# An adaptive-mixing, attention and expert kernel on one core: mixing and transposes in row halves, low parts and the second bound on GpSimd, new instruction orders

## The chip, the core and the metric

The kernel runs on one core of a Trainium2 chip. The core has TensorE (PE: matmuls, with its weight loads shown apart as PEld), VectorE (DVE), ScalarE (ACT), GpSimd (POOL) and SyncE (SP), which here only issues DMAs. Each engine works off its own list of instructions strictly in the written order, and waits at semaphores that other engines count up. The metric is the device time of one execution in microseconds; the median of the runs shown is compared.

## The reference, cut to what matters

The input x has 32 samples of 32 tokens with 512 columns.

```
att  = softmax(MLP(cond_128))                    # 8 shares per sample
x1   = einsum(att-weighted 32x32 weights, x) + bias            # mixing, per sample
q,k,v = x1 @ sign(W).T * (mean|W| * scale)       # 512, 128 and 128 columns, nan_to_num
a    = softmax(q k^T / 4) v                      # 32 heads, 8 kv heads, 32 tokens per sample
y    = a @ sign(Wo).T * (mean|Wo| * scale)       # nan_to_num
x1   = x + y
c    = grouped conv over columns (9 taps) of x1, + context + bias
out  = x1 + experts(c)                           # top 2 of 8 low-rank experts, gated
```

## The kernel before

The 1024 rows (sample, token) are held as 8 tiles t of 128 rows, and in the first part as 4 pairs i of tiles. There is no loop on the chip: each engine's list is written out by hand as calls of small functions, and the order of these calls is the order of the engine's instructions. The stages are:

- Mixing. `mix(i, b)` on TensorE multiplies the rows of x with block-diagonal weights (`agg_diag`); `full_mixed` on VectorE adds the bias into `mixed`; `high_part` on ScalarE rounds it to `mixed_hi`, `low_part` on VectorE takes the rest, `mixed_lo`. The two parts go through TensorE as a pair of quick matmuls where one exact one is wanted.
- Projection. `project_first` (pair 0) and `project(i, b)`; `scale_qkv(i, n)` on ScalarE copies each of six blocks out of PSUM.
- A bound on the numbers. `bound_qkv` on VectorE makes `safe_flag[0]` from sums of absolute values, and `guard_qkv` branches on it; with a safe flag it is one tiny memset. `bound_o` does the same for the output projection: it needs the output scales `o_scale_bc`, which come by way of DRAM. `o_scales` on VectorE writes them, SP stores them (`store_o_scale`, 512 numbers of 4 bytes) and then loads them spread over all partitions (`spread_o_scale`, 256 KB). `scale_y` branches on the second flag.
- Attention of tile t. `spread_keys`, `score`, `row_tops`, `shift_rows`, `exponents`, `row_totals`, `row_inverses`, `normalise` (GpSimd), `turn_probs(t, h)` (a transpose on TensorE for each half h of the heads), `copy_probsT` (ScalarE), `attend`, `attn_high` (ScalarE), `attn_low` (VectorE), `project_out`, `scale_y`.
- Residual and convolution. `residual(t)` on GpSimd for t below 6, `residual_late` on VectorE for 6 and 7; `store_x1(t)` from ScalarE's queue writes the tile to DRAM; `to_window(t)` on SP reads it back with three DMAs of 256 KB in another layout; `convolve`, `bias_conv`, `turn_conv`, `copy_convT`.
- Experts. `ffn_up`, `gate_top`, `gate_masks`, `gate_weights`, `gate_apply`, `turn_gated`, `copy_gatedT`, `ffn_down`, `finish`, `store`.

`turn_probs` of every tile uses one PSUM bank, so each turn waits until ScalarE has copied the last one out:

```
def turn_probs(t, h):
    pe.wait_ge(probs_ready, 2 * t + h + 1)
    reached(pe, probsT_copied, 2 * t + h)
```

## Time and profile before

| | |
|---|---|
| median of 3 runs | 124.25 us (123.92 to 126.06) |
| profiled execution | 124.09 us |
| its span in the trace | 122.3 us |
| TensorE busy | 109.3 us (89%) |
| VectorE busy | 98.0 us (80%) |
| ScalarE busy | 63.2 us (52%) |
| GpSimd busy | 48.7 us (40%) |
| DMA, all queues | 19.56 MB |

The times of instructions are microseconds from the span's start. The profiled execution's own time is 1.8 us more than its span. A number such as L1372 is a line of the kernel before. An fp32 matmul stands as two records in the trace, an fp32 transpose or a rounded (fp32r) matmul as one. "Busy" of TensorE counts overlapping matmuls once; a share of busy time says little of what the end waits for, and the chain of waits and the idle times are what to read.

### The profile page before, as it was taken

The page shows a single profiled execution, that of the slowest core. Times are in us where ns is not written, and L with a number is a line of the kernel's source. Part 1 is how long each engine was busy: PE and PEld are TensorE (multiplying, and loading weights), DVE is VectorE, ACT ScalarE, POOL GpSimd, SP SyncE. Part 2 cuts the span into 40 slices and gives each one's busy share as a digit, 9 for nine tenths or more (in the row PEclk, how much of TensorE's full clock was granted, in tenths as well). Part 3 has the DMA queues.
Part 4 walks back from the last instruction along what each step waited for, and adds up shares of the span by engine and source line. Part 5 has one row for each costly group of instructions (what it writes and reads, how often), then busy time and mean ns, then how long its engine had stood idle before and what let it go on. Part 6 is the DMA issues. An engine that isn't in the chain of part 4 may idle for free.

```text
span 122.3 us, 2847 instructions
## 1 busy us (share of the span) xinstructions
PE 109.3 (89%) x1008; PEld 83.4 (68%) x1008; DVE 98.0 (80%) x269; ACT 63.2 (52%) x147; POOL 48.7 (40%) x68
## 2 busy tenths in 40 slices
PE   1888999999997999995999999999999998699870
PEld 1765979999997977984887758776575535366510
DVE  0059999969949999979999899998967977379852
ACT  4547779894763878266473544656340302213400
POOL 1115920008206548938857999957600000000000
PEclk9999999999999999999999999999999999999998
DMA  3799999940000002000029869899599969982322
GB/s 81 226 336 411 427 383 411 402 150 3 5 0 1 0 5 86 0 3 5 0 86 180 171 145 201 220 191 189 177 201 191 238 213 201 243 184 88 121 109 113
DMA packets 18847, 19.56 MB, mean 160 GB/s; under 512 B 1488, under 2 KB 14480, under 8 KB 18448
## 3 DMA queue, kind: packets, MB, share of 16 engines
q1 hardware_dynamic: 17680, 17.27, 54.6%
q10 hardware_dynamic: 1152, 2.10, 5.2%
q8 instruction: 8, 0.13, 0.5%
q14 instruction: 7, 0.06, 0.2%
HBM read 15.17 MB, written 4.20 MB: 158 GB/s over the span
## 4 chain that ended last, share of the span: by engine, by line
PE 56%; DMA 24%; DVE 9%; issue 5%; ACT 3%; SPq 1%; DVEq 1%; ACTq 0%
PE bank L1404 10%; PE bank L1289 8%; DMA o_scale_row<-scale_all 7%; DMA x_turned<-x_all 7%; PE bank L1306 5%; PE bank L1360 5%; DMA rows_sb<-x_turned 4%; DMA o_scale_bc<-o_scale_row 4%; PE bank L1372 4%; PE bank L1455 3%; PE bank L1442 3%; PE bank L1420 3%; PE bank L1323 3%; PE bank L1324 3%; PE bank L1391 3%
## 5 line engine op out<-in xcount | busy, mean ns | idle before, releaser
L413 POOL TENSOR_TENSOR probs<-probs,row_inv 128x512 f32<-128x512 f32 x16 | 17.2, 1079 | 12.9 <-DVE row_inv L946 12.6
L1323 PE MATMUL bank<-mixed_hi,qkv_sign 128*128 128x256 f32 x72 | 17.6, 287 | 0.0
L1324 PE MATMUL bank<-mixed_lo,qkv_sign 128*128 128x256 f32 x72 | 16.9, 278 | 0.0
L395 POOL TENSOR_TENSOR keys_diag<-kv,keymask 128x512 f32<-128x512 f32 x8 | 8.4, 1052 | 14.5 <-DVE calm L911 13.7
L1404 PE MATMUL bank<-wo_sign,attn_hi 128*128 128x512 f32 x32 | 13.3, 416 | 0.8 <-DVE attn_lo L952 0.8
L1323 PEld LDWEIGHTS bank<-mixed_hi,qkv_sign 128*128 128x128 f32 x72 | 13.5, 188 | 0.6 <-issue 0.4
L1324 PEld LDWEIGHTS bank<-mixed_lo,qkv_sign 128*128 128x128 f32 x72 | 13.5, 188 | 0.0
L566 ACT ACTIVATE probsT<-bank 128x512 f32<-128x512 f32 x16 | 9.5, 596 | 7.2 <-PE bank L1372 7.2
L560 ACT ACTIVATE probs<-probs 128x512 f32<-128x512 f32 x16 | 10.1, 632 | 5.7 <-DVE probs L936 4.5
L1404 PE MATMUL bank<-wo_sign,attn_lo 128*128 128x512 f32 x32 | 12.6, 393 | 0.0
L930 DVE TENSOR_REDUCE row_max<-bank 128x16 f32<-128x512 f32 x16 | 10.6, 675 | 1.0 <-DVE safe_flag L885 0.7
L1289 PEld LDWEIGHTS bank<-agg_diag,x_all 128*128 128x128 f32 x64 | 9.3, 225 | 2.3 <-issue 2.3
L1442 PEld LDWEIGHTS bank<-ffn_in_sb,woT_sb 128*128 128x128 f32 x64 | 8.2, 190 | 4.0 <-issue 3.4
L1289 PE MATMUL bank<-agg_diag,x_all 128*128 128x128 f32 x64 | 10.4, 317 | 0.6 <-DVE agg_diag L784 0.6
L1372 PE MATMUL bank<-misc_sb,probs 128*128 128x128 f32 x64 | 10.1, 281 | 0.7 <-POOL probs L413 0.6
L942 DVE TENSOR_REDUCE row_sum<-probs 128x16 f32<-128x512 f32 x16 | 10.6, 676 | 0.1
L1360 PE MATMUL bank<-keys_diag,queries 64*128 64x128 f32 x128 | 9.3, 284 | 1.5 <-DVE probs L936 1.5
L936 DVE TENSOR_TENSOR probs<-bank,row_max 128x512 f32<-128x512 f32 x16 | 10.4, 666 | 0.1
L1360 PEld LDWEIGHTS bank<-keys_diag,queries 64*128 64x128 f32 x128 | 7.8, 187 | 2.7 <-issue 2.5
L1455 PE MATMUL bank<-ffn_out_sb,gatedT 128*128 128x512 f32 x16 | 8.6, 621 | 1.0 <-DVE x_all L1028 0.6
L1372 PEld LDWEIGHTS bank<-misc_sb,probs 128*128 128x128 f32 x64 | 7.1, 140 | 3.5 <-issue 1.6
L597 ACT ACTIVATE gatedT<-bank 128x128 f32<-128x128 f32 x8 | 2.2, 278 | 13.7 <-PE bank L1448 13.7
(143 smaller groups left out, 234.8 us busy)
## 6 DMA issues: line engine op xcount, KB each, us to landing
rows_sb<-x_turned SPq DMA_DIRECT2D x18, 256.0 KB, 5.0
x_all<-in_x_rows SPq DMA_DIRECT2D x4, 512.0 KB, 9.1
x_turned<-x_all ACTq DMA_DIRECT2D x8, 256.0 KB, 3.1
out_rows<-x_all SPq DMA_DIRECT2D x8, 256.0 KB, 2.4
qkvT_sb<-in_qkvT SPq DMA_DIRECT2D x4, 384.0 KB, 6.3
rows_sb<-in_qkv_rows SPq DMA_DIRECT2D x1, 1536.0 KB, 10.3
qkv_sign<-x_turned SPq DMA_DIRECT2D x6, 256.0 KB, 6.5
rows_sb<-in_wo_rows SPq DMA_DIRECT2D x1, 1024.0 KB, 13.2
```

The source lines that it names most:

```text
L413: pool.tensor_tensor(probs[:, t % 2, h, :, :], probs[:, t % 2, h, :, :], row_inv[:, t % 2, h, :].unsqueeze(2).to_broadcast([P, HALF, TOKENS]),
L930: v.tensor_reduce(row_max[:, t % 2, h, :], scores, AX_X, ALU.max).then_inc(max_ready, 1)
L936: v.tensor_tensor(probs[:, t % 2, h, :, :], scores, row_max[:, t % 2, h, :].unsqueeze(2).to_broadcast([P, HALF, TOKENS]), ALU.subtract).th ...
L942: v.tensor_reduce(row_sum[:, t % 2, h, :], probs[:, t % 2, h, :, :], AX_X, ALU.add).then_inc(sum_ready, 1)
L1289: last = mm(ps_mixed[b][:, at:at + P], x_all[:, 2 * i + a, ph * STEPS:(ph + 1) * STEPS], agg_diag[:, 2 * i + a, :, :].rearrange("p q o -> ...
L1323: mm(dst, w, mixed_hi[:, ph, cols(i % 2, PAIR)], start=(ph == 0 and n % 2 == 0), stop=False)
L1324: last = mm(dst, w, mixed_lo[:, ph, cols(i % 2, PAIR)], start=False, stop=(ph == PHASES - 1 and n % 2 == 1))
L1360: last = mm(ps_scores[h][:, s * P:(s + 1) * P], queries[rows, PER_TILE * t + s, :, :], keys_diag[rows, t % 2, s, :, :].rearrange("p g k -> ...
L1372: last = nc.tensor.transpose(ps_probsT[:, s * P:(s + 1) * P], probs[:, t % 2, h, HEADS * s:HEADS * (s + 1), :], ident)
L1404: last = mm(ps_y[:, :], part[:, t % 2, j, :, :], wo_sign[:, j, :], start=(j == 0 and part is attn_hi), stop=(j == MEMBERS - 1 and part is ...
L1442: last = mm(ps_ffn(t)[:, 0:FFN_COLS], convT[t % 2][:, ph, :, :], ffn_in_sb[:, ph, :], start=(ph == 0), stop=(ph == PHASES - 1))
L1455: mm(ps_down[:, :], gatedT[:, t % 2, :], ffn_out_sb[:, :], start=True, stop=True).then_inc(ffn_done, 1)
```

## The change

1. Mixing of pairs 1 to 3: each matmul over 128 rows becomes two over 64 rows, with 64 output columns each, into two PSUM banks; `full_mixed` then reads a bank for the row half rather than for the phase, and both banks must be done before the first is read. `high_part` waits for both.
2. `turn_probs` of tiles 3 to 6 and `turn_conv` of tiles 3 to 7: four transposes of 128x128 become eight of 64 rows, in two banks; one copy on ScalarE reads both banks. To make this possible the eight banks are one tensor, placed so that pairs are neighbours.
3. The low parts of pairs 2 and 3 move from VectorE to GpSimd (`late_low_part`).
4. `bound_o` moves: the sum over the scales to ScalarE (`sum_o_scales`), five operations on single numbers to GpSimd (`bound_on_output`). VectorE keeps the load of the flag.
5. `attn_high` and `attn_low` do one operation of 512 columns where they did two of 256.
6. The residual of tile 6 moves from VectorE to GpSimd.
7. The order of calls is new on every engine; the windows of tiles 6 and 7 stand ahead of the first stores of the output.

```diff
+            def late_low_part(i, b):
+                pool.wait_ge(hi_ready, 2 * i + b + 1)
+                pool.wait_ge(qkv_done, 3 * (i - 1))
+                pool.tensor_tensor(mixed_lo[:, 2 * b:2 * b + 2, cols(i % 2, PAIR)], mixed[:, 2 * b:2 * b + 2, :],
+                                   mixed_hi[:, 2 * b:2 * b + 2, cols(i % 2, PAIR)].bitcast(F32),
+                                   ALU.subtract).then_inc(late_lo_ready, 1)
+
+            def bound_on_output():
+                pool.wait_ge(bound_ready, 6)
+                pool.tensor_scalar(of_all, of_qkv, of_qkv, 4.0 * DIM, ALU.mult, ALU.mult).then_inc(bound_o_ready, 1)
+                pool.wait_ge(o_scales_summed, 1)
+                pool.tensor_scalar(of_y, of_qkv, by_o, float(HIDDEN), ALU.mult, ALU.mult).then_inc(bound_o_ready, 1)
+                pool.wait_ge(bound_o_ready, 2)
+                pool.tensor_tensor(of_all, of_all, of_y, ALU.add).then_inc(bound_o_ready, 1)
+                pool.wait_ge(bound_o_ready, 3)
+                pool.tensor_tensor(of_all, of_all, of_qkv, ALU.add).then_inc(bound_o_ready, 1)
+                pool.wait_ge(bound_o_ready, 4)
+                pool.tensor_scalar(safe_flag[:, 1:2], of_all, FINITE_BOUND, None, ALU.is_le).then_inc(bound_o_ready, 1)
...
+            def sum_o_scales():
+                act.wait_ge(o_scale_ready, 16)
+                nc.scalar.activation(junk_o[:, :], o_scale_bc[0:1, :], ACT.Abs, accum_out=by_o).then_inc(o_scales_summed, 1)
...
@@ turn_probs (TensorE)
+                if t not in HALVED:
+                    for s in range(PER_TILE):
+                        last = nc.tensor.transpose(bank[6][:, s * P:(s + 1) * P],
+                                                   probs[:, t % 2, h, HEADS * s:HEADS * (s + 1), :], ident)
+                    last.then_inc(probsT_done, 2)
+                    return
...
                 for s in range(PER_TILE):
-                    last = nc.tensor.transpose(ps_probsT[:, s * P:(s + 1) * P],
-                                               probs[:, t % 2, h, HEADS * s:HEADS * (s + 1), :], ident)
-                last.then_inc(probsT_done, 1)
+                    for r in range(2):
+                        rows = slice(P // 2 * r, P // 2 * (r + 1))
+                        at = h * PAIR + s * P // 2
+                        last = nc.tensor.transpose(bank[3 if r else 6][:, at:at + P // 2],
+                                                   probs[rows, t % 2, h, HEADS * s:HEADS * (s + 1), :], ident[rows, rows])
+                        if s == PER_TILE - 1:
+                            last.then_inc(probsT_done, 1)
...
@@ mix (TensorE), pairs 1 to 3
-                    pe.wait_ge(mixed_full, 2 * (i - 1) + b + 1)
+                    pe.wait_ge(mixed_full, 2 * i)
+                    for a in tiles:
+                        for ph in (2 * b, 2 * b + 1):
+                            for r in range(2):
+                                rows = slice(P // 2 * r, P // 2 * (r + 1))
+                                at = (2 * ph + a) * P // 2
+                                last = mm(ps_mixed[r][:, at:at + P // 2], x_all[rows, 2 * i + a, ph * STEPS:(ph + 1) * STEPS],
+                                          agg_diag[rows, 2 * i + a, 2 * r:2 * r + 2, :].rearrange("p q o -> p (q o)"),
+                                          start=True, stop=True)
...
@@ attn_low (VectorE), and attn_high (ScalarE) in the same way
-                for odd in range(2):
-                    dve.wait_ge(attn_hi_ready, 2 * t + odd + 1)
-                    v.tensor_tensor(part_of(attn_lo, t, odd), attn_of(t, odd), part_of(attn_hi, t, odd).bitcast(F32),
-                                    ALU.subtract).then_inc(attn_lo_ready, 1)
+                dve.wait_ge(attn_hi_ready, t + 1)
+                v.tensor_tensor(part_of(attn_lo, t), attn_of(t), part_of(attn_hi, t).bitcast(F32),
+                                ALU.subtract).then_inc(attn_lo_ready, 1)
...
@@ bound_o (VectorE)
-                dve.wait_ge(o_scale_ready, 16)
-                v.tensor_reduce(by_o, o_scale_bc[0:1, :], AX_X, ALU.add, apply_absolute_value=True).then_inc(bound_o_ready, 1)
...
                 dve.wait_ge(bound_o_ready, 5)
-                v.tensor_scalar(safe_flag[:, 1:2], of_all, FINITE_BOUND, None, ALU.is_le).then_inc(bound_o_ready, 1)
-                dve.wait_ge(bound_o_ready, 6)
                 return dve.value_load(safe_flag[0:1, 1:2], min_val=0, max_val=1)
...
@@ order of SP
+            to_window(6)
+            to_window(7)
             store(0)
-            to_window(6)
             store(1)
-            to_window(7)
```

**Place 1: ScalarE, the exponents of tiles 0 and 1 and the first copies of turned probabilities.** L560 is `exponents`, L566 `copy_probsT`, L550 and L556 `scale_qkv`, L542 `high_part`. Before:

```order
L560 ACTIVATE probs<-probs 128x512
L556 ACTIVATE kv<-bank3,scale_v 128x256
L550 ACTIVATE queries<-bank2,scale_all 128x8x32
L542 ACTIVATE mixed_hi<-mixed 128x2x256
L566 ACTIVATE probsT<-bank6 128x512
L550 ACTIVATE queries<-bank2,scale_all 128x8x32
L560 ACTIVATE probs<-probs 128x512
L542 ACTIVATE mixed_hi<-mixed 128x2x256
L566 ACTIVATE probsT<-bank6 128x512
```

In the changed kernel (L612 is `exponents`, L623 `copy_probsT`, L602 `scale_qkv`, L589 `sign_wo`, L594 `high_part`, L633 `attn_high`, L628 the new `sum_o_scales`):

```order
L602 ACTIVATE queries<-halves,scale_all 128x8x32 x2
L589 ACTIVATE wo_sign<-woT_sb 128x512
L612 ACTIVATE probs<-probs 128x512
L628 ACTIVATE junk_o,bound<-o_scale_bc 1x512
L623 ACTIVATE probsT<-halves 128x512
L589 ACTIVATE wo_sign<-woT_sb 128x512
L612 ACTIVATE probs<-probs 128x512
L623 ACTIVATE probsT<-halves 128x512
L594 ACTIVATE mixed_hi<-mixed 128x2x256
L633 ACTIVATE attn_hi<-halves 128x4x4x32
```

The sum over the output scales now stands between the exponents of the first half of tile 1 and the first copy of turned probabilities. The exponents of the second half, the high parts of pair 3 and the attention's high part of tile 0 stand behind it.

**Place 2: VectorE, from the first guard to the output scales (L896, L899) of the changed kernel.** L859 is `full_mixed`, L850 `own_weights(3)`, L876 `sum_rows`, L989 `row_tops`.

```order
L859 TENSOR_TENSOR mixed<-halves,aggb_bc 128x8x64
L850 TENSOR_TENSOR agg_diag<-agg,quadmask 128x256
L876 TENSOR_REDUCE scale_in<-rows_sb 128x1
L859 TENSOR_TENSOR mixed<-halves,aggb_bc 128x8x64
L896 TENSOR_SCALAR scale_in<-scale_in 128x4
L899 TENSOR_TENSOR scale_all<-scale_in,misc_sb 128x4
L989 TENSOR_REDUCE row_max<-halves 128x16 x2
```

Before, `o_scales` stood behind the tops and shifts of tile 0 (L930, L936) and the copy of the convolution's weights (L972):

```order
L930 TENSOR_REDUCE row_max<-bank4 128x16
L930 TENSOR_REDUCE row_max<-bank5 128x16
L936 TENSOR_TENSOR probs<-bank4,row_max 128x512
L936 TENSOR_TENSOR probs<-bank5,row_max 128x512
L972 COPY conv_w_sb<-bank6 96x128
L825 TENSOR_SCALAR scale_in<-scale_in 128x4
L828 TENSOR_TENSOR scale_all<-scale_in,misc_sb 128x4
L799 TENSOR_TENSOR mixed_lo<-mixed,mixed_hi 128x2x256
L942 TENSOR_REDUCE row_sum<-probs 128x16
```

**Place 3: GpSimd, where the second bound went** (L440 is `normalise`, L422 `spread_keys`, L447 `late_low_part`, L453 to L461 `bound_on_output`), in the changed kernel:

```order
L432 TENSOR_TENSOR vals_diag<-values_t,valmask 128x512 x2
L440 TENSOR_TENSOR probs<-probs,row_inv 128x512
L422 TENSOR_TENSOR keys_diag<-kv,keymask 128x512
L440 TENSOR_TENSOR probs<-probs,row_inv 128x512
L453 TENSOR_SCALAR bound<-bound 1x1
L455 TENSOR_SCALAR bound<-bound 1x1
L457 TENSOR_TENSOR bound<-bound 1x1
L459 TENSOR_TENSOR bound<-bound 1x1
L461 TENSOR_SCALAR safe_flag<-bound 1x1
L422 TENSOR_TENSOR keys_diag<-kv,keymask 128x512
L440 TENSOR_TENSOR probs<-probs,row_inv 128x512
L447 TENSOR_TENSOR mixed_lo<-mixed,mixed_hi 128x2x256 x2
```

The bound stands ahead of the keys of tile 3 and the first `normalise` of tile 1, and the late low parts of pair 3 stand behind that.

## Rows read from the trace of the kernel before

**Rows 1.** The page: TensorE busy, and the span in 40 slices

```profile
PE 109.3 (89%) x1008; PEld 83.4 (68%) x1008; DVE 98.0 (80%) x269; ACT 63.2 (52%) x147; POOL 48.7 (40%) x68
...
DMA  3799999940000002000029869899599969982322
```

**Rows 2.** The chain of waits (start us, us, what) in the first 18 us

```profile
9.69 1.19 PE bank L1289 x4
...
12.03 2.86 PE bank L1289 x12
...
16.22 1.09 PE bank L1289 x8
```

**Rows 3.** The timeline (start us, us, ...), VectorE, 27 to 29 us

```profile
27.38 0.42 DVE L784 TENSOR_TENSOR agg_diag<-agg,quadmask 128x256 f32<-128x256 f32 x1 [0.95 <-DVE safe_flag L869]
27.74 0.06 DVE L911 MEMSET calm<- 1x1 f32 x1
```

**Rows 4.** The chain of waits, 32 to 56 us

```profile
32.70 1.78 PE bank L1289 x16
...
35.40 0.17 DVE scale_in L825
...
35.78 8.17 DMA o_scale_row<-scale_all
43.97 5.03 DMA o_scale_bc<-o_scale_row
49.02 0.67 DVE bound L875
...
51.99 0.32 DVEq L887
```

**Rows 5.** The timeline, ScalarE, 38.8 to 42 us

```profile
39.59 0.60 ACT L566 ACTIVATE probsT<-bank 128x512 f32<-128x512 f32 x1 [0.28 <-PE bank L1372]
...
40.91 0.63 ACT L560 ACTIVATE probs<-probs 128x512 f32<-128x512 f32 x1 [0.36 <-DVE probs L936]
```

**Rows 6.** The timeline, TensorE, 41 to 58 us

```profile
41.28 0.60 PE L1372 MATMUL bank<-misc_sb,probs 128*128 128x128 f32 x4
...
56.77 1.16 PE L1360 MATMUL bank<-keys_diag,queries 64*128 64x128 f32 x16 [1.48 <-DVE probs L936]
```

**Rows 7.** The chain of waits, 57 to 61 us

```profile
57.94 0.59 PE bank L1372 x4
...
60.37 0.44 PE bank L1372 x4
```

**Rows 8.** Groups of instructions (busy us, mean ns | idle before)

```profile
L413 POOL TENSOR_TENSOR probs<-probs,row_inv 128x512 f32<-128x512 f32 x16 | 17.2, 1079 | 12.9 <-DVE row_inv L946 12.6
...
L1323 PEld LDWEIGHTS bank<-mixed_hi,qkv_sign 128*128 128x128 f32 x72 | 13.5, 188 | 0.6 <-issue 0.4
...
L930 DVE TENSOR_REDUCE row_max<-bank 128x16 f32<-128x512 f32 x16 | 10.6, 675 | 1.0 <-DVE safe_flag L885 0.7 <-PE bank L1360 0.3
...
L419 POOL TENSOR_TENSOR x_all<-x_all,o_out 128x512 f32<-128x512 f32 x6 | 7.6, 1270 | 2.2 <-DVE o_out L960 2.1
...
L799 DVE TENSOR_TENSOR mixed_lo<-mixed,mixed_hi 128x512 fp32r<-128x512 f32 x8 | 6.1, 764 | 0.1
...
L952 DVE TENSOR_TENSOR attn_lo<-bank,attn_hi 128x256 fp32r<-128x256 f32 x16 | 5.9, 411 | 0.0
```

**Rows 9.** Line 1360, its weight loads (duration ns min/median/max)

```profile
L1360 PEld LDWEIGHTS bank<-keys_diag,queries x128: 182/188/188, 29.5 to 75.0; 64*128 64x128 f32 x128
```

**Rows 10.** The timeline, ScalarE, 61 to 62 us

```profile
61.66 0.34 ACTq L587 DMA_DIRECT2D x_turned<-x_all  x1
```

**Rows 11.** The timeline, TensorE, 94 to 106 us

```profile
94.54 0.27 PE L1448 MATMUL bank<-misc_sb,gated 128*128 128x128 f32 x1
...
105.14 1.07 PE L1420 MATMUL bank<-rows_sb,conv_w_sb 96*32 96x512 f32 x8 [1.15 <-DMA rows_sb<-x_turned]
```

**Rows 12.** A stretch at the end: busy us by engine, PEclk, DMA share

```profile
120.50:121.50 1.00, 0.00 (x0) 0.00 (x0) 0.00 (x0) 0.00 (x0) 0.00 (x0) 0.86 0.67 262
```

More of the change, by code:

```diff
@@ L637, in _ @@
             exponents(0, 1)
-            scale_qkv(1, 5)
             scale_qkv(2, 0)
+            scale_qkv(2, 1)
+            sign_wo(2)
+            exponents(1, 0)
+            sum_o_scales()
+            copy_probsT(0, 0)
+            sign_wo(3)
+            exponents(1, 1)
+            copy_probsT(0, 1)
             high_part(3, 0)
-            copy_probsT(0, 0)
-            scale_qkv(2, 1)
-            exponents(1, 0)
+            attn_high(0)
+            scale_qkv(2, 2)
             high_part(3, 1)
-            copy_probsT(0, 1)
@@ L829, in o_scales @@
                                 ALU.mult).then_inc(scale_ready, 1)
-            x_sum, of_mixed, of_qkv, by_o, of_y, of_all = (bound[:, n:n + 1] for n in range(PAIRS + 4, PAIRS + 10))
+            x_sum, of_mixed = bound[:, PAIRS + 4:PAIRS + 5], bound[:, PAIRS + 5:PAIRS + 6]
             def sum_mix_weights():
@@ L1425, in turn_conv @@
                 pe.wait_ge(conv_biased, t + 1)
-                for s in range(PER_TILE):
-                    last = nc.tensor.transpose(ps_conv(t)[:, s * P:(s + 1) * P], conv_y[t % 2][:, s, :], ident)
-                last.then_inc(convT_done, 1)
+                if t < CONV_HALVED:
+                    for s in range(PER_TILE):
+                        last = nc.tensor.transpose(ps_conv(t)[:, s * P:(s + 1) * P], conv_y[t % 2][:, s, :], ident)
+                    last.then_inc(convT_done, 2)
+                    return
+                if t == CONV_HALVED:
+                    pe.wait_ge(shifted, 2 * TILES)
+                elif t == LATE_TILES[0]:
+                    pe.wait_ge(probsT_copied, 2 * TILES)
+                else:
+                    pe.wait_ge(convT_copied, t - 1)
+                for s in range(PER_TILE):
+                    for r in range(2):
+                        rows = slice(P // 2 * r, P // 2 * (r + 1))
+                        last = nc.tensor.transpose(conv_homes(t)[r][:, s * P // 2:(s + 1) * P // 2], conv_y[t % 2][rows, s, :],
+                                                   ident[rows, rows])
+                        if s == PER_TILE - 1:
+                            last.then_inc(convT_done, 1)
             def ffn_up(t):
@@ L1559, in _ @@
             ffn_up(4)
+            turn_conv(5)
             ffn_down(3)
```

431 lines of the change are left out of this document (226 added, 205 removed).

## Prediction

> **What bounds the kernel now.** I read the page first [rows 1]: TensorE is busy for 89% of the span and VectorE for 80%, in nearly every slice from 8 us on, so no engine is free enough that cutting its work alone settles the end. Then the chain of waits. It runs through TensorE from 9.69 us to 35 us. From 35.4 it goes through the output scales: two tiny operations on VectorE, a store of 512 numbers that lands after 8.17 us, a load that lands after 5.03 us, then six small steps of the second bound on VectorE from 49.02 until the flag is loaded at 52.3 [rows 4]. This delays `shift_rows` of tile 3, and TensorE idles 1.48 us before the scores of tile 4 [rows 6]. From 56.8 to 94.5 the chain is almost all TensorE. Behind that the windows' DMAs are the other limit: the DMA line of the page stands at 8 or 9 in most slices from 64 to 107 us [rows 1], and TensorE waits 1.15 us for the window of tile 6, whose convolution starts at 105.14 [rows 11]; from its start it takes 14.0 us to the last matmul and 3.2 more to the end of the span.
>
> **The output scales, and who waits for them.** This is the term that I put first. `sum_o_scales` is now in ScalarE's list between the exponents of tile 1, half 0 and the first copy of turned probabilities. When do the scales arrive? The first guard was at 27.74 [rows 3]. I put it at 28.3: the bound now comes behind a mixing call and a row sum, while the 0.95 us of the flag's load remains [rows 3]. Then VectorE does two operations of 512 columns at 0.68 (the size of L930 [rows 8]), own_weights at 0.42 [rows 3], a row sum at 0.68 and two tiny ones at 0.17 [rows 4]: 2.8 us, so 31.1, with waits 31.3. The two DMAs have the same form and the same idle queue as before: 31.3 + 8.17 + 5.03, and 0.1 for issuing, is 44.6 [rows 4]. The sum over 512 numbers with its read of the accumulator is near 0.85 (0.67 on VectorE [rows 4]), so ScalarE is free at 45.5. And when does ScalarE get there? Before, it ran that exponent from 40.91 to 41.5 [rows 5]. Nothing ahead of it is later now, and the work removed from VectorE brings it forward; I put it at 39.4. So ScalarE stands still for 3.2 us (old pace) to 5.2 us (mine). TensorE's second turn needs the copy of the first one out of the same bank. It started at 41.28 [rows 6] and starts now at 45.5 + 0.6 (the copy [rows 5]) = 46.1: **4.8 us later**. GpSimd stands still too, in front of `bound_on_output`, and behind it wait the keys of tile 3, a normalise and the late low parts of pair 3, each near 1.1 us: they end at about 51.7, just ahead of the projection of pair 3 at 55.
>
> **What is given back up to the scores of tile 4.** Four low parts leave VectorE, 4 x 0.76 = 3.1 [rows 8], and the bound with its six operations, 49.02 to 51.99, 2.9 [rows 4]. So VectorE no longer holds TensorE up there. Before, TensorE took 16.7 us from 41.28 to the end of those scores at 57.94 [rows 6, 7], with some 2.0 us of idle time (1.48 of it in [rows 6]), and with one turn (0.44) that is now behind them. What remains is 14.2; I add 0.4 because `turn_values(2)` now stands ahead of the tops of tile 3. The scores end at 46.1 + 14.6 = 60.7, **+2.8** instead of +4.8. The shorter `attn_low` is one operation for two of 0.41 [rows 8]: near 0.68, 0.14 each, 1.1 in all on VectorE and about as much on ScalarE, mostly beside TensorE's work. GpSimd gets 4 x 1.1 to 1.27 of low parts, 5 tiny ones and one residual of 1.27 [rows 8], 7 us on a base of 48.7 [rows 1]: I find room for it before 56 us and after 76.
>
> **The halves.** A turn of four transposes takes 0.44 us, or 0.58 right behind row-split matmuls [rows 7]. Eight halves at 64 columns, two at a time, could take 0.22 plus 0.1 to 0.2 of changing over, and where the turn stands next to `score`, which is row-split itself, no change-over at all. I take 0.2 saved for each of the eight turns of tiles 3 to 6, 1.6, and 0.15 for each convolution's, 0.75. The ends are 0 (the loads don't overlap) and 0.3. Mixing is different. An exact call takes 0.89 (two of them 1.78 [rows 4]). The nearest row-split group of 16 records, the scores, takes 1.09 to 1.16 [rows 6], with 128 columns each where there are now 64. So a halved call lies between 0.45 (half of 0.89) and 1.1; I take 0.95, because a weight load of 64 rows has 188 ns [rows 9] and so may set the pace. Four calls lie ahead of the first guard: -1.8 to +0.8 us on TensorE there, but the scales' date hangs on ScalarE's copies as well, so at most -0.9 on it.
>
> The Trainium skill ("TensorE: Matmul & The Clock Gate", the section on LDWEIGHTS) says that a load's time follows the columns loaded and not the rows. The trace agrees: the loads of 64 rows behind the scores take 188 ns and those of 128 rows in the projection take 188 as well [rows 8, 9]. By that rule halved mixing would save nothing, by plain halving 0.45 a call.
>
> **From the scores of tile 4 to the end.** From 57.94 to 94.54, where the last `project_out` ends [rows 7, 11], TensorE took 36.6 us. Now the same list plus one turn (+0.44), minus 1.6 for halves, minus 0.4 of waits that the lighter VectorE ends: 35.6 with rounding up. It ends at 96.3, +1.8. The convolution of tile 6 could have started at 103.99 but for its window [rows 11]; now 104.0 + 1.8 - 0.6 for halved turns = 105.2. The window itself: stores of x1 now leave at once where ScalarE held the first until 61.66 [rows 10], and no output store goes ahead of windows 6 and 7, but the residual of tile 6 takes 1.27 instead of 0.69, so I leave it at 105. Behind it the list has one turn more and the up-projection of tile 7 earlier: 14.0 again. **The stall alone gives +0.1 on the span**: 122.4, and with the 1.8 around it 124.2.
>
> **The clock.** TensorE idles from about 41.4 to 46.1. At the program's end the granted clock was still full until near 121.2, 2.1 us after the last matmul, and half after it: a mean of 0.86 from 120.5 to 121.5 [rows 12]. At the start the same mixing matmuls took 0.24 each until 14.9 and 0.11 from 16.2 on [rows 2], after 6.5 us of steady work. So after 4.7 us of idleness I expect 1.2 GHz instead of 2.4 for 2 to 6.5 us, which costs half of that, 1.0 to 3.2, less what TensorE would have waited for ScalarE anyway. I take +1.5. The forecast is 122.4 + 1.5 + 1.8 = **125.6 us** (this profiled execution was 124.1, the median 124.25, so they need no correction).
>
> **Rivals.**
> - No stall: the scales arrive by the time that ScalarE is there, or it gets there later than I think. For it: the edit moves their start 4 us ahead. Against it: 8.17 and 5.03 [rows 4]. Then TensorE runs through from 30 us, the scores of tile 4 end near 55.8, all stores and windows are some 4.8 us earlier, and the time is 124.1 - 4.8 = **119.3**. The Trainium skill ("DMA: Bandwidth & Descriptors", the anatomy of one DMA, told there for GpSimd's path) gives a DMA a fixed part of about 2 us. By it, an estimate, the scales would come at about 36 and nobody would wait; the trace contradicts it for these two.
> - The stall, but a clock that stays high: **124.2**.
> - Slower: the low clock lasts 6.5 us as at the start [rows 2] and nothing of it hides. It costs 3.2 instead of 1.5: **127.4**. It decides from about 5 us of low clock on.
> - The halves don't do what they say: if pairs of transposes don't overlap, eight at 0.11 take 0.88 instead of 0.44, 13 turns cost +5.7 on TensorE instead of -2.3: 130. Against it, the scores' pairs do overlap: 16 records in 1.16 [rows 6].
>
> **How the numbers follow.** Stall with a low clock of middling length 0.43; stall at full clock 0.16; low clock long 0.10; no stall 0.27; halves that don't overlap 0.04. Within 2% (121.8 to 126.7), which is about what a measurement of this kernel can tell from no change, lie most of the first two: 0.45. Slower: the third, the fifth and the upper part of the first, 0.23. Faster: 0.32, nearly all "no stall". The range must reach to both signs, 118.6 to 127.6; the forecast's own is 123.5 to 127.
>
> **What would show it.** Right: ScalarE idle for 3 to 5 us before the sum over the scales, released by the DMA `o_scale_bc`; TensorE idle for some 4.7 us before the second turn, and records at double length behind it; VectorE free of waits at tile 3. Halved turns at 0.2 to 0.35 a group, halved mixing at 0.85 to 1.1. Wrong: the DMA lands before 40, or ScalarE reaches the sum after 44; then it is 119. If a halved mixing call takes 0.5, take 0.5 to 1 off everything.

## The result, and the profile after

The changed kernel takes **133.22 us** (median of 4 runs, 131.92 to 136.89) against 124.33 us: ratio 1.064, 95% interval 1.057 to 1.071. Here and below a ratio and its interval compare only executions within 1.5% of the fastest of their kernel, while a median and a range take in all. The prediction was 125.6 us, range 118.6 to 127.6. The profiled execution took 131.92 us, its span is 130.1.

TensorE comes to full speed at a date that differs between executions: six kernels below whose lists are the same up to the first guard (the memset of `calm`; changed, e1, e2, e4, f1, g3) reached it at 19.4 to 28 us in their traces, and their guards came at 31.2 to 35.4, half a us later for each us. There is one trace for each kernel, so that this is also what spreads the times of one kernel (by 0.5 to 5.5 us) is likely and not shown. Stretches below are therefore counted from the first guard.

The page after, lines as in [rows 1] and the clock's line:

```profile
PE 113.7 (87%) x1108; PEld 84.8 (65%) x1108; DVE 91.2 (70%) x250; ACT 64.2 (49%) x141; POOL 55.3 (42%) x78
...
PE   1979999999999508999999999989999989798970
...
PEclk9999999999999965799999999999999999999997
DMA  3899999800100020000059259699699949991233
```

VectorE has 6.8 us less work than before, as planned, and TensorE has a hole in the slices from 42 to 49 us with the granted clock down behind it. The chain of waits there (start us, us, what), to be read beside [rows 4]:

```profile
33.89 0.16 DVE scale_in L896
...
34.27 8.73 DMA o_scale_row<-scale_all
...
43.02 4.80 DMA o_scale_bc<-o_scale_row
...
47.84 0.72 ACT junk_o L628 x2
48.56 0.49 ACT probsT L623
49.05 0.14 issue
49.19 1.09 PE halves L1438 x4
```

ScalarE's timeline says who stands there: the copy (L623) that TensorE's second turn needs is behind the sum over the scales (L628). GpSimd's bound waits at the same place:

```profile
41.26 0.63 ACT L612 ACTIVATE probs<-probs 128x512 f32<-128x512 f32 x1
47.84 0.63 ACT L628 ACTIVATE junk_o<-o_scale_bc 1x512 f32<-1x512 f32 x1 [5.95 <-DMA o_scale_bc<-o_scale_row]
```

```profile
48.66 0.26 POOL L455 TENSOR_SCALAR bound<-bound 1x1 f32<-1x1 f32 x1 [5.46 <-ACT junk_o L628]
```

The second turn starts at 49.19 and not at 41.28 [rows 6], 7.9 us later. TensorE has idled 5.02 us. The granted clock fell to the lower of its two levels, 1.2 GHz, near 46.6 and stayed there until about 53.4 (columns: busy us of PE, PEld, DVE, ACT, POOL; then PEclk):

```profile
44.00:46.00 2.00, 0.16 (x4) 0.02 (x2) 1.29 (x2) 0.00 (x0) 0.00 (x0) 1.00 0.02 9
46.00:48.00 2.00, 0.00 (x0) 0.00 (x0) 0.00 (x0) 0.16 (x1) 0.00 (x0) 0.65 0.31 122
48.00:50.00 2.00, 0.81 (x4) 0.72 (x4) 0.00 (x0) 2.00 (x5) 1.01 (x5) 0.50 0.00 0
50.00:52.00 2.00, 2.00 (x18) 1.79 (x16) 0.69 (x1) 1.20 (x3) 2.00 (x3) 0.50 0.03 8
52.00:54.00 2.00, 2.00 (x41) 1.41 (x38) 1.29 (x2) 0.55 (x2) 1.09 (x1) 0.64 0.00 0
```

The start lost time too. The first guard is at 31.24 where it was at 27.74 [rows 3]:

```profile
31.24 0.06 DVE L970 MEMSET calm<- 1x1 f32 x1 [1.49 <-ACT queries L602]
```

TensorE's timeline, 14 to 22 us: matmuls run at half speed until about 19.4 (12 of line 1371 take 2.88 here and 1.6 later), where the kernel before was through by 16.2 [rows 2].

```profile
14.60 2.08 PE L1322 MATMUL halves<-probs,ones 32*128 32x256 f32 x4
16.61 2.88 PE L1371 MATMUL halves<-mixed_hi,qkv_sign 128*128 128x256 f32 x12
19.41 2.00 PE L1345 MATMUL halves<-agg_diag,x_all 64*128 64x64 f32 x32
```

The halves, from the chain: a halved turn (L1448) takes 0.39 to 0.46 against 0.44 to 0.59 [rows 7], and scores beside it 0.95 instead of 1.09.

```profile
70.33 0.39 PE halves L1448 x8
70.72 0.95 PE halves L1425 x16
...
71.69 0.46 PE halves L1448 x8
```

The end, from the chain: x1 of tile 6 is stored and its window loaded, the convolution of tile 6, and the last three `ffn_down` (L1544), the last two of them each behind a `finish` on VectorE:

```profile
99.08 6.33 DMA x_turned<-x_all
...
106.30 5.12 DMA rows_sb<-x_turned
...
111.46 1.07 PE halves L1494 x8
...
122.03 0.96 PE halves L1544 x2
...
123.86 1.11 PE halves L1544 x2
...
125.83 1.11 PE halves L1544 x2
```

### The profile page after: what moved, and what is told of

It reads as the page before. It is cut to its first block, busy times and chain, and to the rows that moved or that the text cites. A ratio compares the mean times of both kernels' runs of the same rounds, so it can differ in the third digit from the quotient of the medians.

```text
span 130.1 us, 3037 instructions
## 1 busy us (share of the span) xinstructions
PE 113.7 (87%) x1108; PEld 84.8 (65%) x1108; DVE 91.2 (70%) x250; ACT 64.2 (49%) x141; POOL 55.3 (42%) x78
## 4 chain that ended last, share of the span: by engine, by line
PE 52%; DMA 21%; DVE 8%; issue 8%; ACT 5%; POOL 2%; POOLq 1%; SPq 1%; DVEq 0%; ACTq 0%
PE halves L1478 8%; DMA o_scale_row<-scale_all 7%; PE halves L1371 5%; DMA x_turned<-x_all 5%; PE halves L1425 5%; DMA rows_sb<-x_turned 4%; PE halves L1544 4%; DMA o_scale_bc<-o_scale_row 4%; PE halves L1531 3%; PE halves L1388 3%; PE halves L1354 3%; PE halves L1345 3%; PE halves L1389 3%; PE halves L1465 3%; PE halves L1322 2%
## 5 line engine op out<-in xcount | busy, mean ns | idle before, releaser
L440 POOL TENSOR_TENSOR probs<-probs,row_inv 128x512 f32<-128x512 f32 x16 | 16.7, 1049 | 3.6 <-DVE row_inv L1005 3.4
L1388 PE MATMUL halves<-mixed_hi,qkv_sign 128*128 128x256 f32 x72 | 17.7, 289 | 0.0
L1389 PE MATMUL halves<-mixed_lo,qkv_sign 128*128 128x256 f32 x72 | 16.9, 278 | 0.0
L422 POOL TENSOR_TENSOR keys_diag<-kv,keymask 128x512 f32<-128x512 f32 x8 | 8.5, 1070 | 16.0 <-DVE calm L970 15.9
L1388 PEld LDWEIGHTS halves<-mixed_hi,qkv_sign 128*128 128x128 f32 x72 | 13.6, 189 | 0.9 <-issue 0.6
L1389 PEld LDWEIGHTS halves<-mixed_lo,qkv_sign 128*128 128x128 f32 x72 | 13.6, 189 | 0.0
L1478 PE MATMUL halves<-wo_sign,attn_hi 128*128 128x512 f32 x32 | 13.4, 418 | 0.0
L1478 PE MATMUL halves<-wo_sign,attn_lo 128*128 128x512 f32 x32 | 12.6, 393 | 0.0
L612 ACT ACTIVATE probs<-probs 128x512 f32<-128x512 f32 x16 | 10.1, 630 | 4.5 <-DVE probs L995 3.7
L989 DVE TENSOR_REDUCE row_max<-halves 128x16 f32<-128x512 f32 x16 | 10.4, 665 | 2.5 <-PE halves L1425 2.5
L995 DVE TENSOR_TENSOR probs<-halves,row_max 128x512 f32<-128x512 f32 x16 | 10.6, 676 | 0.3 <-PE halves L1438 0.2
L1425 PE MATMUL halves<-keys_diag,queries 64*128 64x128 f32 x128 | 10.1, 301 | 0.5 <-DVE probs L995 0.3
L1531 PE MATMUL halves<-ffn_in_sb,woT_sb 128*128 128x136 f32 x64 | 9.5, 291 | 0.9 <-ACT gatedT L662 0.9
L1544 PE MATMUL halves<-ffn_out_sb,gatedT 128*128 128x512 f32 x16 | 8.7, 623 | 1.2 <-DVE x_all L1087 1.2
L623 ACT ACTIVATE probsT<-halves 128x512 f32<-128x512 f32 x8 | 4.8, 595 | 6.5 <-PE halves L1438 6.5
```

The lines of the kernel that those rows point to most:

```text
L440: pool.tensor_tensor(probs[:, t % 2, h, :, :], probs[:, t % 2, h, :, :], row_inv[:, t % 2, h, :].unsqueeze(2).to_broadcast([P, HALF, TOKENS]),
L612: nc.scalar.activation(probs[:, t % 2, h, :, :], probs[:, t % 2, h, :, :], ACT.Exp, scale=float(DIM) ** -0.5).then_inc(exp_ready, 1)
L989: v.tensor_reduce(row_max[:, t % 2, h, :], scores, AX_X, ALU.max).then_inc(max_ready, 1)
L995: v.tensor_tensor(probs[:, t % 2, h, :, :], scores, row_max[:, t % 2, h, :].unsqueeze(2).to_broadcast([P, HALF, TOKENS]), ALU.subtract).th ...
L1388: mm(dst, w, mixed_hi[:, ph, cols(i % 2, PAIR)], start=(ph == 0 and n % 2 == 0), stop=False)
L1389: last = mm(dst, w, mixed_lo[:, ph, cols(i % 2, PAIR)], start=False, stop=(ph == PHASES - 1 and n % 2 == 1))
```

## The experiments

All stretches in one table, from each kernel's profiled execution, in us. "Full speed": where matmul records change from double to single length. "Turn 2": start of the second turn of probabilities; "scores": end of `score(4)`; "out": end of the last `project_out`; all three from the guard. Then from "out" to the convolution of tile 6 (conv 6), from that to the end of the span, and from the guard to the end. Each row is one execution. How far such stretches repeat is seen in four variants of the kernel before (f3, g4, h2, h3, under "The start"), whose lists behind the guard are those of the kernel before: 93.9 to 94.0 us from guard to end against its 94.6, with most of the difference between out and conv 6.

| kernel | full speed | guard | turn 2 | scores | out | to conv 6 | to end | guard to end |
|---|---|---|---|---|---|---|---|---|
| before | 16 | 27.7 | 13.5 | 30.2 | 67.0 | 10.4 | 17.2 | 94.6 |
| changed | 19.4 | 31.2 | 18.0 | 33.7 | 70.5 | 9.7 | 18.6 | 98.9 |
| e1 sum and bound later | 21 | 32.0 | 12.9 | 28.9 | 65.7 | 9.9 | 18.7 | 94.3 |
| e2 clock held | 28 | 35.4 | 18.0 | 32.0 | 68.7 | 9.6 | 18.6 | 96.9 |
| e3 old start orders | 27 | 34.8 | 17.7 | 34.1 | 70.9 | 9.2 | 18.6 | 98.7 |
| e4 old end | 25.6 | 34.3 | 18.0 | 33.8 | 70.6 | 10.0 | 17.3 | 97.9 |
| f1 = e1 + e4 | 25.6 | 34.3 | 12.8 | 28.9 | 67.3 | 9.3 | 17.3 | 93.9 |
| f2 = f1, full mixing | 21.5 | 31.5 | 16.1 | 32.8 | 70.5 | 9.2 | 17.4 | 97.0 |
| f4 = f2, early work | 19.8 | 30.6 | 14.6 | 30.7 | 68.9 | 9.2 | 17.4 | 95.4 |
| g1 = e4, early scales | 19.3 | 30.9 | 12.6 | 26.6 | 63.3 | 9.4 | 17.3 | 90.0 |
| g2 = g1, full mixing | 22 | 31.6 | 12.2 | 26.1 | 62.9 | 9.2 | 17.3 | 89.3 |
| g3 only ScalarE's sum later | 25.6 | 34.1 | 12.9 | 32.5 | 69.2 | 9.8 | 18.7 | 97.6 |
| h1 = g2, old start | 21 | 30.3 | 14.0 | 27.9 | 64.7 | 9.2 | 17.3 | 91.2 |
| i1 = h1, sum a step later | 16 | 27.8 | 12.8 | 26.7 | 63.5 | 9.2 | 17.3 | 90.0 |
| i2 only early scales | 25.8 | 33.9 | 12.8 | 26.7 | 63.4 | 9.1 | 18.6 | 91.1 |

**e1_late_sum.** ScalarE's sum and GpSimd's bound moved behind the work that waited for them.

```diff
 @@ ScalarE
-            sum_o_scales()
             copy_probsT(0, 0)
...
             scale_qkv(2, 3)
+            sum_o_scales()
 @@ GpSimd
-            bound_on_output()
             spread_keys(3)
...
             spread_keys(4)
+            bound_on_output()
```

> The changed kernel (132 us) with two calls later: ScalarE sums the output scales after the fourth copy of pair 2 and not ahead of the first copy of turned probabilities, GpSimd's bound follows the fifth spread of keys. Theory A (the wait for the scales is most of the loss): the scales still land near 47.8 us, but the second turn of probabilities comes near 44.2 instead of 49.2, TensorE's clock stays full (2.0 us), score(4) ends near 58 to 59 instead of 65.0, and the time is 125 to 127.5. Theory B (the start and the end are most of it, and VectorE and GpSimd would have been late in the middle anyway): the time falls by less than 2.5 us, to 129.5 or more.

128.97 us (128.05 to 131.3), ratio 1.043 (1.019 to 1.067). The second turn comes 12.9 us after the guard instead of 18.0, and guard to end is 4.6 us shorter. The time lies between the two theories, and a new wait stands in the trace: VectorE now waits 3.48 us for the late bound, and TensorE 2.04 us for the shifts behind it.

```profile
54.17 0.69 DVE L1001 TENSOR_REDUCE row_sum<-probs 128x16 f32<-128x512 f32 x1 [3.48 <-POOL safe_flag L461]
```

```profile
59.79 1.16 PE L1425 MATMUL halves<-keys_diag,queries 64*128 64x128 f32 x16 [2.04 <-DVE probs L995]
```

**e2_hold_clock.** The stall stays; TensorE gets five matmuls of 512 columns in it, whose results nobody reads.

```diff
             mix(3, 1)
+            hold_clock(5)
             turn_probs(0, 1)
```

> The changed kernel with the stall left as it is, and five matmuls of 512 columns into a free bank, whose results nobody reads, ahead of the second turn of probabilities. Theory A (the clock that falls in the stall is a loss of its own): the granted clock stays full from 46 to 54 us, the matmuls behind the stall take half as long, and the time falls by 1.5 to 2.2 us to 130 to 130.5. Theory B (the work behind the stall waits for VectorE and GpSimd whatever the clock): less than 0.5 us.

133.02 us (130.37 to 134.23): as a median no better than the changed kernel, and theory A's 130 to 130.5 was met only by the fastest execution. The profiled one (134.23) came to full speed only at 28 us; the others have no trace. From the guard, the turn is as late as before (18.0) but the scores end 1.7 us and the last `project_out` 1.8 us earlier, with the granted clock full throughout:

```profile
48.00:50.00 2.00, 2.00 (x12) 1.17 (x11) 1.29 (x3) 0.00 (x0) 0.00 (x0) 1.00 0.03 5
50.00:52.00 2.00, 2.00 (x6) 0.85 (x5) 0.00 (x0) 0.00 (x0) 0.00 (x0) 1.00 0.48 126
```

So the fallen clock is 1.7 to 1.8 us of the loss.

**g3_late_act_sum.** One wait of the two.

```diff
 @@ ScalarE, as in e1; GpSimd as changed
-            sum_o_scales()
             copy_probsT(0, 0)
```

> The changed kernel with ScalarE's sum of the scales later, as in the kernel with the late sum, but with GpSimd's bound where the change put it. Theory A (either of the two waits is enough for most of the loss): GpSimd waits from 11.7 us after the guard until the scales have landed and are summed (17 us after it), the normalisation of tile 1 behind it is late, and from the guard to score(4) it takes 32 us or more (33.7 with both waits, 28.9 with none). Theory B (ScalarE's wait alone did the harm): 30 us or less.

133.35 us, ratio 1.074 (1.063 to 1.085). GpSimd waits 5.91 us, `normalise` of tile 1 is late, and TensorE now idles at the turn after it:

```profile
55.26 0.66 PE L1438 MATMUL halves<-misc_sb,probs 128*128 128x128 f32 x4 [3.84 <-POOL probs L440]
```

The scores end 32.5 us after the guard, against 33.7 with both waits and 28.9 with neither in e1: GpSimd's wait alone keeps most of the loss. ScalarE's alone was not tried.

**g1_early_scales** and **i2_only_early_scales.** The other way round: the places stay, the scales come sooner. i2 has nothing but this; g1 also the old end.

```diff
 @@ ScalarE
             scale_qkv(0, 1)
+            sum_rows(BLOCKS + 0, 3)
+            sum_rows(BLOCKS + 2, 4)
             scale_qkv(0, 2)
 @@ VectorE
+            sum_rows(BLOCKS + 1)
+            sum_rows(BLOCKS + 3)
             keep_scale_v()
+            o_scales()
             safe_qkv = bound_qkv()
```

> The changed kernel with the old order of the end, and with the output scales computed ahead of the first guard (their four row sums in idle time of ScalarE and VectorE) instead of 2.8 us behind it. ScalarE's sum and GpSimd's bound stand where the change put them. Theory A (only the date of the scales is wrong, the places of the sum and the bound would do): the scales land about 13.6 us after they are computed, near the first guard + 11.5 us, ScalarE waits under 1.5 us, the second turn of probabilities comes 12.9 to 14 us after the guard instead of 18, VectorE has no wait for the bound either (3.5 us in the kernel with the late sum), and from the first guard to the end it takes 91 to 93 us against 93.9 in the kernel with the late sum and the old end. Theory B (the store slows down or queues among the last weight loads, which still run then): the scales land as late as before, 97 us.

> The changed kernel with nothing but the output scales computed ahead of the first guard; the end stays in its new order. Theory A (that the scales land 5 us too late for the places of the sum and the bound is 7 to 8 us of the 8.9 us that the change lost): 123.5 to 125.5 us, from the first guard to the end 91 to 91.5 us (90.0 with the old end, plus 1.3). Theory B: over 127 us.

g1: 123.63 us (122.71 to 125.61), ratio 0.996 (0.985 to 1.007). i2: 126.11 us (123.78 to 129.06), ratio 1.000 (0.994 to 1.006) beside a kernel before of 126.45. In both the scales are computed 2.3 us ahead of the guard (in g1 at 28.67, guard at 30.93); ScalarE waits 0.32 us in g1 and 0.51 in i2. From g1, VectorE and ScalarE:

```profile
28.67 0.16 DVE L899 TENSOR_TENSOR scale_all<-scale_in,misc_sb 128x4 f32<-128x4 f32 x1
...
41.65 0.63 ACT L628 ACTIVATE junk_o<-o_scale_bc 1x512 f32<-1x512 f32 x1 [0.32 <-DMA o_scale_bc<-o_scale_row]
```

i2 takes 7.8 us off the stretch from guard to end (98.9 to 91.1) by moving five calls. With the late sum, 2.3 us of this were not to be had: there the flag came late for VectorE.

**e4_old_tail** and **f1_late_sum_old_tail.** The order from the last `project_out` on as before; f1 has e1's edit as well.

```diff
             turn_gated(5)
-            ffn_down(4)
-            ffn_up(7)
+            turn_conv(7)
             ffn_down(5)
+            ffn_up(7)
             turn_gated(6)
```

> The changed kernel with the old order from the last project_out on, on TensorE, ScalarE and VectorE (homes and row halves as changed; the residual of tile 6 stays on GpSimd). Theory A (the new order of the end costs 1.5 us): from conv(6) to the end 17.2 us instead of 18.6, the time falls by 1.2 to 1.8 us, to 130.2 to 130.8. Theory B (the longer end comes from halves and homes, not from order): less than 0.4 us.

> The changed kernel with both edits at once: the sum of the output scales and the bound later, and the old order from the last project_out on. The date at which TensorE reaches full speed at the start differs between executions by several us, so stretches are counted from the first guard (from it to the end: 94.6 us in the kernel before, 98.9 in the changed one, 94.3 with the late sum alone, and the old end alone took 1.3 off the stretch behind conv(6)). Theory A (the two losses are independent): 93.0 us from the first guard to the end, 17.3 of them behind conv(6). Theory B (the old end only helps because it is late): 94 or more.

e4: 133.65 us (131.87 to 135.33), ratio 1.072 (1.040 to 1.105); f1: 130.08 us (126.35 to 130.56). In every kernel with the old end it is 17.2 to 17.4 us from conv 6 to the end, in every one with the new end 18.6 or 18.7: 1.3 us, whatever else is changed. f1 as a whole missed its 93.0 (93.9). Its stretch up to the scores equals e1's, but TensorE's idle 2.05 us there brought the clock down, and e1's 2.04 us did not. f1, then e1:

```profile
62.00:64.00 2.00, 1.93 (x21) 1.84 (x22) 1.88 (x4) 1.32 (x3) 2.00 (x2) 0.84 0.02 4
64.00:66.00 2.00, 2.00 (x11) 2.00 (x11) 1.98 (x5) 1.77 (x4) 2.00 (x3) 0.50 0.34 131
```

```profile
60.00:62.00 2.00, 2.00 (x26) 1.88 (x25) 1.88 (x4) 1.40 (x4) 2.00 (x3) 1.00 0.10 38
62.00:64.00 2.00, 2.00 (x19) 1.96 (x18) 1.72 (x6) 2.00 (x6) 2.00 (x3) 1.00 0.25 98
```

**f2_full_mixing**, **f4_full_mixing_warm**, **g2_early_full_mixing.** Matmuls, additions and high parts of pairs 1 to 3 in full rows; f4 also has three matmuls of ones ahead of the first layer and one more matmul ahead of the first mixing.

```diff
-                    pe.wait_ge(mixed_full, 2 * i)
+                    pe.wait_ge(mixed_full, 2 * (i - 1) + b + 1)
...
-                            for r in range(2):
```

> The previous kernel with mixing in full rows again (matmuls, additions and high parts as in the kernel before; GpSimd's late low parts and everything else stay). Theory A (the halved mixing is what makes the first guard late beyond the late full speed): the guard ends 1.5 to 1.8 us earlier at the same date of full speed (near 28 for full speed at 16.3, half a us later for each us of delay), and the stretch from the guard to score(4) stays 29 us. The time falls by 1.5 to 2 us. Theory B (the halved mixing costs only its longer matmuls, 0.07 to 0.1 a call): the guard 0.4 us earlier.

> The kernel with the late sum, the old end and full mixing, with the same early work for TensorE. If the parts that are kept (low parts and the bound on GpSimd, merged attn_low, turns in row halves, the new order of the middle) are worth something: from the first guard to the end 92.5 to 93.2 us against 94.6 in the kernel before. Theory A of the warm start: full speed before 14 us and 120.5 to 122 us in all; theory B: no change to the kernel without the early work.

> The same with full mixing. In the two kernels with full mixing and late scales, VectorE's two operations of 4 columns on the scales took 1.07 and 1.20 us instead of 0.15, while GpSimd computed its late low parts. Theory A (VectorE's small operations were held up by GpSimd's): ahead of the guard, where GpSimd is idle, both take 0.2 us or less, and the second turn of probabilities comes within 14 us of the guard instead of 14.6 and 16.1; the guard itself comes 0.9 us earlier than with halved mixing for the same date of full speed; guard to end 91 to 93 us. Theory B (the additions in full rows are what delays the middle): over 14.5 us from the guard to the second turn.

f2: 130.43 us, ratio 1.056 (1.046 to 1.067); f4: 129.14 us (127.75 to 131.93); g2: 122.64 us, ratio 0.990 (0.982 to 0.998). Compared at one date of full speed (half a us for each us of it), the guard comes 0.8 us earlier: less than theory A and more than B. But f2's second turn came 3.3 us later after the guard than f1's, f4's 1.8 us later. VectorE's two operations of four columns on the scales took 1.07 and 1.20 us instead of 0.15 and 0.16, and each ended when one of GpSimd's low parts ended (35.2 and 36.45):

```profile
34.15 1.07 DVE L891 TENSOR_SCALAR scale_in<-scale_in 128x4 f32<-128x4 f32 x1
35.26 1.20 DVE L894 TENSOR_TENSOR scale_all<-scale_in,misc_sb 128x4 f32<-128x4 f32 x1
```

```profile
33.91 2.54 POOL L447 TENSOR_TENSOR mixed_lo<-mixed,mixed_hi 128x512 fp32r<-128x512 f32 x2
```

TensorE waited 2.27 us for the shifts behind them, in f2 and in f4 alike. f4 kept its clock. In f2 it fell, and the slower matmuls make up the rest of f2's delay (columns as above):

```profile
39.00:42.00 3.00, 3.00 (x20) 2.78 (x21) 2.61 (x8) 2.05 (x5) 2.17 (x3) 0.50 0.00 0
```

In g2 they run ahead of the guard, with GpSimd idle, in 0.17 and 0.16, and the turn comes after 12.2 us. In the changed kernel they fell by luck into a gap of GpSimd (0.15 at 33.89).

**The start.** e3 has the old start orders with halved mixing. f3 and g4 are the kernel before with more and with less early work on TensorE, h2 the kernel before in the new PSUM places, h3 the kernel before with TensorE's new start order:

```diff
             mix(0, 0, (0,))
-            mix_bias_first()
             mix(0, 1, (0,))
+            mix_bias_first()
...
-            mix(1, 0)
             project_first(mixed_hi, 0)
+            mix(1, 0)
```

> The changed kernel with the start in the old order on TensorE, ScalarE and VectorE, up to the first guard (the halved mixing of pairs 1 to 3 stays, and the first halved addition of pair 2 stays behind the guard). Theory A (the new order of the start makes the guard late and keeps the matmuls at half speed until 20 us): the matmuls are at full speed from 16.3 us, the guard ends near 28.5 instead of 31.2, the scales land near 45, and the time falls by 2 to 3 us, to 129 to 130. Theory B (the late rise of the speed has nothing to do with the order, or what is won is lost again): the full speed comes near 20 us as before, less than 1 us in all.

> The kernel before with TensorE kept at work from 1 us on: three 128-column matmuls of ones ahead of the first layer, and one more where it waits for the first mixing weights; their results are read by nobody. Theory A (full speed comes after a time of steady work, and the early gaps put it off): full speed comes before 14 us in the profiled run, the time falls by 1 to 3 us to 121.5 to 123, and the runs lie closer together than 123.1 to 128.1. Theory B (its date has nothing to do with the work, it varies from execution to execution): full speed anywhere from 16 to 28 us, times as of the kernel before.

> The kernel before without the three matmuls that keep TensorE at work while it waits for the shares of the mixes. The two profiled runs of the kernel before and of the one with more early work reached full speed at 16.3 and 16.0 us, the eight of the changed kernel and its relatives at 20 to 28. Theory A (the early work sets the date): full speed later than 18 us and 1 to 5 us more in all. Theory B (it does not): full speed near 16 us and no change in time, or a date that is as late as in the changed kernel's runs by chance.

> The kernel before with only the places in PSUM changed: one tensor of all banks, and the eight tiles in the banks that the change gives them. Theory A (the order of the start decides the date of full speed, the banks nothing): full speed near 16 us, 123 to 124.5 us. Theory B (something of the banks, as an eviction or a matmul that meets another in a neighbouring one, decides): full speed at 20 us or later, and 1.5 to 4 us more.

> The kernel before with only TensorE's order of the start changed to the new one (full mixing stays). Up to 14.6 us TensorE does the same work in both orders. Theory A (the new order decides the date of full speed): full speed at 20 us or later, the first guard at 29.5 or later, 125.5 to 128 us. Theory B (it does not): full speed at 16 us in the profiled run, guard within 0.7 us of 27.7, 123.5 to 125 us.

| kernel | us | full speed | guard |
|---|---|---|---|
| e3 | 135.24, ratio 1.089 (1.067 to 1.111) | 27 | 34.8 |
| f3 | 125.17, ratio 1.004 (0.997 to 1.011) | 16 | 27.7 |
| g4 | 124.03, ratio 0.999 (0.987 to 1.010) | 16 | 27.6 |
| h2 | 123.73 (123.44 to 126.99) | 16 | 27.6 |
| h3 | 127.41 (125.99 to 130.94) | 19.3 | 30.3 |

Early work and places do nothing. Of seven profiled executions with TensorE's old start order five are at full speed by 16 us, h1 at 21 and e3 at 27, so both theories of e3 missed it; of twelve with the new order none is before 19.3. Up to 14.6 us TensorE does the same work in both. h3's lowest of five runs, 125.99, is 2.1 us above the lowest of seven runs of the kernel before beside it (123.86). That the new order shuts out the early date fits all of this, but with one trace for each kernel it is not proven; why it should, no run here shows. For one date of full speed, the new orders cost the guard 0.8 us with full mixing (h3 and g2 against i1 and h1), but only some 0.3 with halved mixing (e4 against e3).

**h1_old_start_early_scales** and **i1_later_sum.** Everything that was worth something at once: old start (with full mixing) and old end, new middle, early scales. i1 then moves the sum behind the exponents of tile 1 and GpSimd's bound behind the keys of tile 3.

```diff
 @@ h1, in bound_qkv on VectorE, behind the six steps of the bound
+                o_scales()
                 dve.wait_ge(bound_ready, 6)
 @@ i1, ScalarE
-            sum_o_scales()
             copy_probsT(0, 0)
             sign_wo(3)
             exponents(1, 1)
+            sum_o_scales()
             copy_probsT(0, 1)
 @@ i1, GpSimd
-            bound_on_output()
             spread_keys(3)
+            bound_on_output()
```

> Everything of the changed kernel from the first guard to the last project_out, with the start of the kernel before (orders of TensorE, ScalarE and VectorE, full mixing), the old order of the end, and the output scales computed ahead of the first guard (VectorE's sum of the last mixing weights follows the guard in their place). Theory A (the start of the kernel before is what lets TensorE reach full speed at 16 us): full speed at 16 us, guard at 28.1, 89.5 to 90.5 us from there to the end, 119.3 to 120.5 us in all against 124. Theory B (the date of full speed is a matter of the execution): it falls anywhere between 16 and 28 us, and the time is 121 to 124. Either way ScalarE waits up to 1.5 us for the scales, since they are read from 39 us on and land near 40.

> The kernel with the old start and the early scales, with ScalarE's sum of the scales one exponential later and GpSimd's bound behind the fourth spread of keys. Theory A (the 1.85 us that ScalarE waited for the scales there cost TensorE its wait of 1.06 us): from the first guard to the end 90 us instead of 91.2, and in executions that reach full speed at 16 us 119 to 120 us in all, 3 to 4% under the kernel before. Theory B (the wait moves to VectorE's additions of pair 3): within 0.3 us of that kernel.

h1: 122.98 us (120.16 to 123.24), at full speed only at 21 us in its profiled execution; only its fastest execution is near theory A's 119.3 to 120.5. i1: **119.42 us (118.88 to 122.09), ratio 0.955 (0.948 to 0.963)**: the best version, under both kernels. Not all of it is the date of full speed (16 us in its profiled execution, as in the kernel before): guard to end it is 90.0 against 94.6. ScalarE no longer waits for the scales, and GpSimd waits 0.62 us for the sum:

```profile
PE 108.2 (92%) x1060; PEld 81.8 (70%) x1060; DVE 91.2 (78%) x250; ACT 63.3 (54%) x141; POOL 55.3 (47%) x78
...
PEclk9999999999999999999999999999999999999999
```

```profile
40.62 0.63 ACT L628 ACTIVATE junk_o<-o_scale_bc 1x512 f32<-1x512 f32 x1
```

## Why the prediction was wrong, step by step

The mechanism of the stall was right: ScalarE and GpSimd stand in front of the output scales. Its place, its releaser, TensorE's idle time (5.02 us, 4.7 predicted) and the fallen clock behind it are in the trace. What failed first is the date of the first guard, to which the whole sum is tied; behind the stall, the stretch to the last `project_out`, the window of tile 6 and the end were each taken 1.0 to 1.5 us too short. In the order of the prediction's sum, with its clock term included from the second turn on:

- **The first guard, 28.3.** It came at 31.24. This step failed most: +2.9 us, carried to the end. Against the kernel before it is 3.5 late. About 1.9 of it is the late full speed (half of some 15.5 to 19.4; the four matmul records of the bias in front of 16.2 took 1.40 us before and 2.08 here), which the sum did not have at all: I took the rise at 16.2 [rows 2] for fixed. The other 1.6 is halved mixing together with the order of the start: some 0.8 for the halves (f2, f4), which I let range down to a gain of 0.9, and some 0.8 for the order (h3). The split depends on what stands beside it (e3 puts some 0.3 on the order), the sum does not. Why full speed came late stays open.
- **Scales 2.8 to 3.0 us after the guard, then 13.3 for the two DMAs.** 2.84 us, and 13.6 from the first issue to the last landing (8.73 + 4.80): right.
- **ScalarE at the sum at 39.4.** 41.9, late by the same start. The stall was 5.95, beyond my 5.2, since the scales landed 3.2 later than I put them and ScalarE came 2.5 later.
- **From the second turn to the scores of tile 4, 14.6 and 1.5 for the clock.** 15.8: the clock cost 1.7 to 1.8 (e2) and the rest was 14.0. Right; the rival at full clock (124.2) had the wrong size of clock, and the one with the long low clock (3.2) too.
- **From there to the last `project_out`, 35.6.** 36.6, exactly as before. My own terms (36.6 + 0.44 - 1.6 - 0.4) come to 35.0; "rounding up" to 35.6 hid a part of this. The halved turns are 0.05 to 0.2 shorter in the chain and not always 0.2, but each `score` beside them is 0.14 shorter too. The 0.4 of waits did not go but grew: TensorE idles 0.9 us in this stretch against 0.4, longest 0.44 and 0.23 ahead of turns of the convolution, for `bias_conv` on VectorE. The rest of the gap I did not trace. Halved mixing took 0.97 to 1.04 a call (0.95 predicted, 0.89 before).
- **The convolution of tile 6 at 105.2, since its window is left at 105.** This step failed too: it came at 111.46. x1 of tile 6 was stored at 99.08 and not at 91.02, and the DMAs behind it took 6.33 + 5.12 where they had taken 8.09 + 5.10. The window has no date of its own: it follows the attention (7.4 us of the 8.1 by which the store is late) and the residual, now 1.27 us on GpSimd. From the last `project_out` to the convolution it took 9.9 us after 10.6; of the 1.7 us that I gave back there, 0.7 came.
- **14.0 us behind it, "again".** 15.5. The new order bunches `ffn_down` 5 to 7 behind `finish`; with the old one it is 14.1 again (e4).

In sum +2.8, +1.0, +1.0 and +1.5 on 123.8 of span make 130.1. Two slips of arithmetic changed nothing: 122.4 + 1.5 + 1.8 is 125.7, and by its own terms the last rival should have been at 132 (124.2 and 8.0 more), not 130.

"No stall" got 0.27 and 119.3. That the change alone would do it was never near: the scales landed 5.9 us after they were wanted. The changed kernel without the stall is i2, and it ties with the kernel before. That i1 takes 119.4 does not confirm the price, since i1 also undoes the start, the halved mixing and the end; here the two numbers agree by luck.

What the change was worth without the stall shows in i2 and g1: guard to end 91.1 and 90.0 against 94.6 before and 98.9 in the changed kernel. Up to the scores of tile 4 the new middle with early scales gains 3.6 us (26.6 in g1 against 30.2), and the stall cost 7.1 of the 33.7 there. The start cost 3.5 and the end 1.3.

## What to carry to other kernels

Before a small reduction is moved onto an engine that works in strict order, follow its input back through every DMA and date its arrival; here two DMAs took 13.6 us, and computing the input 5 us earlier was worth 8 us, while moving the waiters later was worth 4 to 5. Price a stall with the clock behind it, and measure stretches between events of the same execution where the start varies. Don't treat a transfer as a fixed date if its source moves with the work that you delay.

## What the hardware showed that I had not expected

- Full speed of TensorE at the start comes anywhere from 16 to 28 us in these executions, with TensorE at work without a gap from 9.7 us on. The granted clock of the stretches reads 1.00 all the while, so that it must be read from the length of the matmul records. Each us of delay costs half a us (guard at 31.2 for 19.4, at 35.4 for 28).
- 2.04 us of idleness left the clock up (e1), and behind 2.05 us it fell for some 3.5 us (f1); behind 2.27 us it stayed up in f4 and fell in f2. The length of the idle time alone does not decide it.
- Beside GpSimd's low parts, two small VectorE operations between SBUF operands lasted until the GpSimd instruction had ended: 1.07 and 1.20 us for 0.15. The Trainium skill says the same ("SBUF — State Buffer", section "Terms": VectorE and GpSimd share a port pair, held for a full instruction, and the loser blocks), and the trace agrees. A reduction of 512 columns beside GpSimd's work kept its 0.67.
- The store of 512 numbers to DRAM took 8.0 to 8.8 us in every one of the nineteen traces.
